# Last stage of a four-stage kernel: the mask written by ScalarE, and four places of its turn reordered

## Chip, cores and metric

One core of a Trainium2 chip runs the whole kernel. The metric is the device time of one execution in microseconds (us); the time before is the median of three runs.

## What is computed

Four stages run one after the other on an activation of 16 sequences x 256 tokens x 128 channels: a recurrent attention, a gated feed-forward net, a full attention, and, as the last stage, six layers of local attention with a feed-forward net. Only the last stage changes. For each layer and each sequence it does:

```python
x = x + local_attention(shift_tokens(x)) @ Wo       # 16 heads of 64, windows of 32
x = x + ffn(layer_norm(x))                          # gelu gate, 341 hidden
# attention: q, k are L2-normalised and turned by rotary tables; a query of a window sees
# its own window and the one before (64 keys):
mask = (it < jb) | (it > jb + w) | (jb == -1)
sim = where(mask, -max, einsum('bhwie,bhwje->bhwij', bq, bk2) * 8)
attn = softmax(sim);  out = einsum('bhwij,bhwje->bhwie', attn, bv2)
# shift_tokens: the upper 64 channels are moved by one token, with a zero at the first
```

## The kernel before

The last stage works through 96 units (six layers x 16 sequences), called n, in a software pipeline of 100 turns, called f. In one turn each engine runs its own list, written out by hand: the first projections of unit f, the last ones and the norms of f-1, the scores and softmax of f-2, the weighted sum and the residual of f-3, the feed-forward net of f-4. Engines meet through semaphores alone, and each engine runs its list in order, so an instruction that waits holds all that stands behind it.

Channels lie on the partitions. Keys and queries are made in eight chunks (`project`, 128 x 512, in banks 0 and 1 in turn). ScalarE squares each chunk (`squares`), GpSimd adds the two halves (`add_halves`), and a product on TensorE with 0/1 weights sums them (`sum_squares`, bank 7). ScalarE turns the sums into reciprocal roots (`norm_rsqrt`: Ln, Exp, Square), VectorE refines them (`norm_weight`, `norm_factor`, `norm_split`, with `norm_high` on ScalarE between), and TensorE spreads them (`spread_norms`). VectorE multiplies each chunk by the rotary tables (`rotary_products`), GpSimd adds the two products (`rotary_sums`, one for each chunk), and SyncE moves queries and keys into their places by 8 DMAs each (`place_queries`, `place_keys`). `rotary_sums` of chunk 0 waits for the key DMAs of the unit before.

The scores of a unit come in two halves h (`scores`, banks 2 and 3): first the mask is put there by eight bf16 products with an identity, then 64 products add the scores. VectorE takes the maximum (`softmax_maximum`) and subtracts it (`softmax_shift`), which frees the banks. GpSimd scales (`scale_shifted`), ScalarE takes the exponential (`softmax_exp`), VectorE sums, GpSimd divides (`softmax_scale`), VectorE transposes. `token_products` makes the values of eight windows (w = 0 to 7, banks 4 and 5), which ScalarE copies out (`read_products`); product 2 goes to the bank of product 0 and waits until ScalarE has read product 0. `attention` is the weighted sum, in two halves. The tokens pass through bank 6: `read_tokens` copies them shifted to SBUF, `split_high_tokens` rounds them, and `split_low_tokens` on VectorE takes the difference.

At the first unit of a layer, ScalarE also writes the rotary tables (`tables`), four of them between `norm_rsqrt` and `softmax_exp`; two turns later TensorE computes `head_matrices` behind the second half of `attention`.

TensorE's list between its tokens and the token products, before:

```python
ffn_up(f - 4, 0); ffn_up(f - 4, 1); scores(f - 2, 0)
project(f - 1, 5); attention(f - 3, 0); project(f - 1, 6); ffn_up(f - 4, 2)
project(f - 1, 7); scores(f - 2, 1); sum_squares(f - 1, 1); attention(f - 3, 1)
token_products(f - 2, 0); project(f, 0, 1); token_products(f - 2, 1); ...
```

## Time and profile before

| | |
|---|---|
| median of 3 runs | 4238.78 us (4233.77 to 4241.29) |
| the profiled execution | 4246.35 us, of it 4244.5 us span |
| TensorE busy over the span | 3910.8 us (92%), VectorE 3529.0 (83%), ScalarE 2638.6 (62%), GpSimd 2381.6 (56%) |
| last stage | from 1325 us (first projection) to the end |
| dearest lines of TensorE | token products 757.9 us, projections 720.7, scores 403.7, weighted sums 373.6, mask 151.7 |

A line of the profile names an engine, the line of the code, the output and the inputs, and how often it ran. "Idle before" is the time in which the engine had nothing to do before these instructions, and what ended it. In the timeline "x8" are eight instructions merged, and the second number runs from the start of the first to the end of the last; matmuls are pipelined, so the distance between starts says what a group costs. "PEld" is TensorE's loading of weights.

### The profile page before, as it was taken

The page shows a single profiled execution, that of the slowest core. Times are in us where ns is not written, and L with a number is a line of the kernel's source. Part 1 is how long each engine was busy: PE and PEld are TensorE (multiplying, and loading weights), DVE is VectorE, ACT ScalarE, POOL GpSimd, SP SyncE. Part 2 cuts the span into 40 slices and gives each one's busy share as a digit, 9 for nine tenths or more (in the row PEclk, how much of TensorE's full clock was granted, in tenths as well). Part 3 has the DMA queues.
Part 4 walks back from the last instruction along what each step waited for, and adds up shares of the span by engine and source line. Part 5 has one row for each costly group of instructions (what it writes and reads, how often), then busy time and mean ns, then how long its engine had stood idle before and what let it go on. Part 6 is the DMA issues. An engine that isn't in the chain of part 4 may idle for free.

```text
span 4244.5 us, 120128 instructions
## 1 busy us (share of the span) xinstructions
PE 3910.8 (92%) x48128; PEld 2747.8 (65%) x48128; DVE 3529.0 (83%) x5537; ACT 2638.6 (62%) x5550; POOL 2381.6 (56%) x2045
## 2 busy tenths in 40 slices
PE   3457999999995999999999999999999999999998
PEld 1225776767764676667766676667766676667666
DVE  6875556777776899989998899989998899989897
ACT  3543336666664666666667666666666666666665
POOL 0111001000003787878888788878888787878785
PEclk7678999999997999999999999999999999999999
DMA  3000000000001333333332333333332333333332
GB/s 104 0 0 1 1 1 1 1 0 0 0 1 40 76 90 82 69 76 88 78 78 65 79 88 81 70 75 94 73 81 62 81 87 81 71 73 72 91 77 65
DMA packets 264482, 238.94 MB, mean 56 GB/s; under 512 B 31524, under 2 KB 260136, under 8 KB 263208
## 3 DMA queue, kind: packets, MB, share of 16 engines
q1 hardware_dynamic: 263976, 231.82, 23.5%
q8 instruction: 363, 5.95, 0.6%
q14 instruction: 143, 1.17, 0.1%
HBM read 26.20 MB, written 4.19 MB: 7 GB/s over the span
## 4 chain that ended last, share of the span: by engine, by line
PE 73%; DVE 12%; ACT 7%; issue 3%; SPq 2%; POOL 1%; DMA 1%; DVEq 0%; ACTq 0%; POOLq 0%
PE bank L1977 14%; PE bank L1910 13%; PE bank L1995 8%; PE bank L1950 7%; PE bank L2037 5%; PE bank L854 5%; ACT arena L1129 3%; PE bank L2050 2%; PE bank L1943 2%; DVE arena L1016 2%; PE bank L1921 2%; DVE arena L1026 2%; PE bank L1254 1%; SPq L2151 1%; PE bank L1245 1%
## 5 line engine op out<-in xcount | busy, mean ns | idle before, releaser
L1448 DVE TENSOR_TENSOR arena<-bank,tab 128x1024 f32<-128x1024 f32 x768 | 935.5, 1219 | 193.0 <-ACT arena L1680 138.8
L1835 POOL TENSOR_TENSOR arena<-arena 128x512 f32<-128x512 f32 x768 | 1010.7, 1332 | 49.6 <-DMA arena<-arena 44.9
L1680 ACT ACTIVATE arena<-bank 128x512 f32<-128x512 f32 x768 | 457.9, 596 | 538.9 <-PE bank L1910 530.1
L1977 PE MATMUL bank<-m_vo,arena 128*32 128x512 f32 x6144 | 757.9, 599 | 17.4 <-DVE arena L1541 11.1
L1910 PE MATMUL bank<-x_split,wqk_split 128*128 128x256 f32 x4608 | 720.7, 299 | 34.9 <-DVE arena L1448 21.0
L1910 PEld LDWEIGHTS bank<-x_split,wqk_split 128*128 128x128 f32 x4608 | 605.6, 192 | 184.3 <-issue 93.9
L1843 POOL TENSOR_TENSOR arena<-arena 128x256 f32<-128x256 f32 x768 | 558.6, 739 | 159.4 <-ACT arena L1680 158.7
L1704 ACT ACTIVATE arena<-bank 128x512 f32<-128x512 f32 x768 | 456.8, 596 | 186.9 <-PE bank L1977 184.2
L1852 POOL TENSOR_TENSOR arena<-arena 128x1024 f32<-128x1024 f32 x192 | 372.4, 1940 | 263.2 <-DVE arena L1496 263.2
L1187 POOL TENSOR_TENSOR x_all<-x_all,arena 128x256 f32<-128x256 f32 x16 | 11.6, 727 | 836.5 <-DVE arena L1008 836.5
L1858 POOL TENSOR_TENSOR arena<-arena 128x1024 f32<-128x1024 f32 x192 | 373.5, 1946 | 127.0 <-DVE arena L1509 126.7
L1950 PE MATMUL bank<-arena 128*32 128x128 f32 x12288 | 403.7, 273 | 0.0
L1995 PE MATMUL bank<-arena 128*32 128x128 f32 x12288 | 373.6, 274 | 0.6 <-issue 0.5
L1950 PEld LDWEIGHTS bank<-arena 128*32 128x32 f32 x12288 | 345.6, 110 | 36.9 <-issue 0.5
L1995 PEld LDWEIGHTS bank<-arena 128*32 128x32 f32 x12288 | 332.7, 110 | 32.5 <-issue 2.0
L1977 PEld LDWEIGHTS bank<-m_vo,arena 128*32 128x32 f32 x6144 | 159.5, 109 | 260.1 <-ACT arena L1704 140.6
L1129 ACT ACTIVATE arena<-bank,arena 128x256 f32<-128x256 f32 x512 | 235.4, 472 | 130.9 <-DVE arena L1016 128.7
L2037 PE MATMUL bank<-arena,w 128*128 128x256 f32 (+1 forms) x1152 | 282.0, 381 | 0.8 <-ACT arena L1735 0.8
L1516 DVE STREAM_TRANSPOSE arena<-arena 128x1024 f32<-128x1024 f32 x192 | 235.1, 1224 | 25.8 <-POOL arena L1858 25.8
L1490 DVE TENSOR_REDUCE arena<-bank 128x16 f32<-128x1024 f32 x192 | 234.1, 1219 | 12.0 <-PE bank L1950 4.1
L1484 DVE TENSOR_TENSOR arena<-arena,bank 128x1024 f32<-128x1024 f32 x192 | 232.1, 1209 | 3.0 <-PE bank L1932 3.0
L1496 DVE TENSOR_TENSOR arena<-bank,arena 128x1024 f32<-128x1024 f32 x192 | 233.0, 1214 | 0.0
(258 smaller groups left out, 7159.4 us busy)
## 6 DMA issues: line engine op xcount, KB each, us to landing
arena<-arena SPq DMA_DIRECT2D x1536, 128.0 KB, 2.5
wqk_stage<-in_wqk SPq DMA_DIRECT2D x6, 1024.0 KB, 8.6
out_x<-x_all SPq DMA_DIRECT2D x7, 512.0 KB, 6.0
wvt<-in_wvt SPq DMA_DIRECT2D x6, 512.0 KB, 4.4
wo<-in_wo SPq DMA_DIRECT2D x6, 512.0 KB, 5.5
arena<-in_wbh SPq DMA_DIRECT2D x1, 2048.0 KB, 9.7
w<-in_w SPq DMA_DIRECT2D x6, 341.0 KB, 5.9
wqk_stage<-out_x SPq DMA_DIRECT2D x2, 512.0 KB, 5.0
```

Source lines behind the costliest of these rows:

```text
L1448: nc.vector.tensor_tensor(d_t[c % KS].rearrange("p k h t -> p k (h t)"), bank[c % 2][:, :].unsqueeze(1).to_broadcast([P, 2, 2 * T]), tab[: ...
L1680: nc.scalar.activation(d_sq[i % 4].rearrange("p h t -> p (h t)"), bank[c % 2][:, :], ACT.Square).then_inc(s_sq, 1)
L1704: nc.scalar.activation(d_u[:, 1 + w, :, :], bank[U_BANK[w]][:, :].rearrange("p (a c) -> p a c", a=QUADS), ACT.Copy).then_inc(s_uev, 1)
L1835: nc.gpsimd.tensor_tensor(d_rot[i // 4][:, i % 4, :, :], t[:, :, 0, :], t[:, :, 1, :], ALU.add).then_inc(s_ad, 1)
L1843: nc.gpsimd.tensor_tensor(sq[:, 0, :], sq[:, 0, :], sq[:, 1, :], ALU.add).then_inc(s_sa, 1)
L1852: nc.gpsimd.tensor_tensor(e, e, factor.to_broadcast([P, WPT, QUADS, 2 * WIN]), ALU.mult).then_inc(s_rm, 1)
L1858: nc.gpsimd.tensor_tensor(d_e[h], d_e[h], d_inv[h].unsqueeze(2).to_broadcast([P, 4 * QUADS, 2 * WIN]), ALU.mult)\
L1910: last = nc.tensor.matmul(bank[c % 2][:, h * T:(h + 1) * T], wqk_split[:, i, wp, h, :], x_split[:, n % 2, xp, :], start=(q == 0), stop=(q ...
L1950: last = nc.tensor.matmul(bank[2 + b][g * WIN:(g + 1) * WIN, (2 * v + a) * P:(2 * v + a + 1) * P], d_q[:, a, g, at:at + WIN], d_k[:, a, g, ...
L1977: last = nc.tensor.matmul(bank[U_BANK[w]][g * WIN:(g + 1) * WIN, :], d_xt[n % 3][:, w * WIN:(w + 1) * WIN], m_vo[:, 4 * g:4 * g + 4, :].re ...
L1995: last = nc.tensor.matmul(bank[6][v * WIN:(v + 1) * WIN, h * C:(h + 1) * C], d_pt[h][:, at, :], d_u[:, WPT * h + v + z, r, :], start=(r == ...
L2037: last = nc.tensor.matmul(bank[UP_BANK[c]][0:m, half * T:(half + 1) * T], w1_of(n)[:, first + c * P:first + c * P + m], d_xn, start=True, ...
```

## The change

ScalarE writes the mask into the two score banks with one copy of 128 x 1024 for each half, instead of TensorE's eight bf16 products; TensorE's eight products stay for the very first half alone. `scores` now waits for this copy. The copy for half 1 stands in ScalarE's list behind `squares` of chunk 6, that for half 0 of the next unit behind the second `softmax_exp`. `split_low_tokens` reads the tokens from bank 6 (two instructions of 64 partitions, the upper one shifted) and stands second in VectorE's list. `softmax_shift` of half 0 stands ahead of the rotary product of chunk 5, and the last two `ffn_gate` and `residual` move up. On TensorE the second half of `attention` stands ahead of `project` of chunk 7. On ScalarE `squares` of chunk 7 stands behind all of `ffn_gelu`. On GpSimd `add_halves` of chunk 7 stands behind `rotary_sums` of chunk 5 and `scale_shifted` of half 0.

```diff
 def split_low_tokens(n):
     dve.wait_ge(s_xh, n + 1)
-    nc.vector.tensor_tensor(x_split[:, n % 2, 1, :], d_xt[n % 3], x_split[:, n % 2, 0, :].bitcast(F32), ALU.subtract)\
-        .then_inc(s_split, 1)
+    at_least(dve, s_proj, CHUNKS * (n - 1))
+    first, second, now = slice(0, C // 2), slice(C // 2, C), n % 2
+    nc.vector.tensor_tensor(x_split[first, now, 1, :], bank[6][first, 0:T],
+                            x_split[first, now, 0, :].bitcast(F32), ALU.subtract)
+    nc.vector.tensor_tensor(x_split[second, now, 1, 1:], bank[6][second, 0:T - 1],
+                            x_split[second, now, 0, 1:].bitcast(F32), ALU.subtract).then_inc(s_split, 1)
...
 for f in range(TURNS_D):            # VectorE
     turn_probabilities(f - 3, 1)
+    split_low_tokens(f)
     rotary_products(f - 1, 3)
     ffn_gate(f - 4, 0)
     rotary_products(f - 1, 4)
     softmax_maximum(f - 2, 0)
-    rotary_products(f - 1, 5)
     softmax_shift(f - 2, 0)
-    rotary_products(f - 1, 6, 7)
+    rotary_products(f - 1, 5, 6)
     ffn_gate(f - 4, 1)
+    ffn_gate(f - 4, 2)
+    rotary_products(f - 1, 7)
+    residual(f - 3)
     softmax_maximum(f - 2, 1)
-    split_low_tokens(f)
-    ffn_gate(f - 4, 2)
     norm_weight(f - 1)
-    residual(f - 3)
     norm_factor(f - 1)
...
+def write_mask(n, h):               # ScalarE
+    if not here(n) or n == 0 and h == 0:
+        return
+    act.wait_ge(s_sub, 2 * n + h)
+    src = mask_bf[:, :, :, :] if h == 0 else mask_bf[:, 1:2, :, :].to_broadcast([P, TPS, 8, 2 * WIN])
+    nc.scalar.activation(psum[:, 2:4, :].rearrange("p b (a k) -> p b a k", k=2 * WIN), src, ACT.Copy).then_inc(s_mask, 1)
...
     squares(f - 1, 5, 6)
+    write_mask(f - 2, 1)
     ffn_gelu(f - 4, 1)
+    ffn_gelu(f - 4, 2)
     squares(f - 1, 7)
-    ffn_gelu(f - 4, 2)
     nc.scalar.preload_act_table_set(EXP_SET)
     norm_rsqrt(f - 1)
...
     softmax_exp(f - 2, 1)
+    write_mask(f - 1, 0)
     read_products(f - 2, 5)
...
     rotary_sums(f - 1, 4)           # GpSimd
-    add_halves(f - 1, 6, 7)
+    add_halves(f - 1, 6)
     rotary_sums(f - 1, 5)
     scale_shifted(f - 2, 0)
+    add_halves(f - 1, 7)
     rotary_sums(f - 1, 6, 7)
...
 def scores(n, h):                   # TensorE
-    at_least(pe, s_sub, 2 * n + h)
+    if n == 0 and h == 0:
+        for b in range(2):
+            for g in range(4):
+                nc.tensor.matmul(bank[2 + b][g * WIN:(g + 1) * WIN, :], ident_bf[:, g * WIN:(g + 1) * WIN],
+                                 mask_bf[:, min(h + b, 1), :, :].rearrange("p a k -> p (a k)"),
+                                 start=True, stop=True, skip_group_check=True, tile_position=(0, g * WIN))
+    else:
+        pe.wait_ge(s_mask, 2 * n + h)
     for b in range(2):
-        for g in range(4):
-            nc.tensor.matmul(bank[2 + b][g * WIN:(g + 1) * WIN, :], ident_bf[:, g * WIN:(g + 1) * WIN],
-                             mask_bf[:, min(h + b, 1), :, :].rearrange("p a k -> p (a k)"),
-                             start=True, stop=True, skip_group_check=True, tile_position=(0, g * WIN))
...
     project(f - 1, 6)
     ffn_up(f - 4, 2)
+    attention(f - 3, 1)
     project(f - 1, 7)
     scores(f - 2, 1)
     sum_squares(f - 1, 1)
-    attention(f - 3, 1)
```

`attention` of half 0 also waits for `s_split`, since it overwrites bank 6; the elements of the low half that no instruction writes now are set to zero once.

## Rows read from the trace of the kernel before

**Rows 1.** The windows view, one stretch: time, then busy time by engine, granted clock.

```profile
3000.00:3300.00 300.00, 294.83 (x4380) 207.07 (x4378) 269.04 (x329) 204.59 (x389) 240.46 (x206) 0.99 0.32 73
```

**Rows 2.** The chain that ended last, in order of time: start, length, what.

```profile
3008.47 0.33 PE bank L1943 x4
3008.80 0.87 PE bank L1950 x32
3009.67 0.21 PE bank L1943 x4
```

**Rows 3.** TensorE in the timeline: start, length, line, operation; one turn and the next.

```profile
3006.30 0.44 PE L1897 MATMUL bank<-ident,x_all 128*128 128x128 f32 x2
...
3018.15 0.61 PE L1921 MATMUL bank<-arena,sel 128*32 128x256 f32 x8
3018.58 1.92 PE L1995 MATMUL bank<-arena 128*32 128x128 f32 x64
3020.33 1.03 PE L1977 MATMUL bank<-m_vo,arena 128*32 128x512 f32 x8
3021.29 1.69 PE L1910 MATMUL bank<-x_split,wqk_split 128*128 128x256 f32 x12
3022.91 1.92 PE L1977 MATMUL bank<-m_vo,arena 128*32 128x512 f32 x16
3024.77 0.44 PE L2006 MATMUL bank<-ident,x_all 128*128 128x128 f32 x2
...
3035.51 0.44 PE L1897 MATMUL bank<-ident,x_all 128*128 128x128 f32 x2
```

**Rows 4.** GpSimd in the timeline, the starts of two turns.

```profile
3007.04 2.52 POOL L1835 TENSOR_TENSOR arena<-arena 128x512 f32<-128x512 f32 x2
...
3037.09 2.51 POOL L1835 TENSOR_TENSOR arena<-arena 128x512 f32<-128x512 f32 x2 [0.86 <-DMA arena<-arena]
...
3044.65 0.74 POOL L1843 TENSOR_TENSOR arena<-arena 128x256 f32<-128x256 f32 x1
...
3046.64 1.29 POOL L1835 TENSOR_TENSOR arena<-arena 128x512 f32<-128x512 f32 x1
3047.89 1.94 POOL L1852 TENSOR_TENSOR arena<-arena 128x1024 f32<-128x1024 f32 x1
3049.78 2.92 POOL L1835 TENSOR_TENSOR arena<-arena 128x512 f32<-128x512 f32 x2
```

**Rows 5.** The waits, whole last stage: total us, times, longest.

```profile
POOL arena L1835 <- DMA arena<-arena: 44.9, 55, 5.1
```

**Rows 6.** ScalarE in the timeline, the same turn.

```profile
3002.10 1.04 ACT L1696 ACTIVATE arena<-arena 128x1024 f32<-128x1024 f32 x1
3004.29 0.60 ACT L1704 ACTIVATE arena<-bank 128x512 f32<-128x512 f32 x1 [1.15 <-PE bank L1977]
...
3008.16 1.28 ACT L1789 ACT_TABLE_LOAD   x1
3009.45 0.47 ACT L1743 ACTIVATE arena<-bank,cols_d 128x256 f32<-128x256 f32 x1
...
3018.83 0.39 ACT L1688 ACTIVATE arena<-bank 128x256 f32<-128x256 f32 x1 [0.51 <-PE bank L1921]
...
3020.65 1.06 ACT L1696 ACTIVATE arena<-arena 128x1024 f32<-128x1024 f32 x1 [0.54 <-POOL arena L1852]
3022.31 0.60 ACT L1680 ACTIVATE arena<-bank 128x512 f32<-128x512 f32 x1 [0.59 <-PE bank L1910]
...
3023.11 0.59 ACT L1704 ACTIVATE arena<-bank 128x512 f32<-128x512 f32 x1
```

**Rows 7.** Groups of instructions, whole last stage: count, busy us, mean ns, idle before.

```profile
L1436 DVE TENSOR_TENSOR x_split<-arena,x_split 128x256 fp32r<-128x256 f32 x96 | 128.5, 1338 | 0.4 <-ACT x_split L1664 0.4
...
L1523 DVE TENSOR_TENSOR x_all<-x_all,bank 128x256 f32<-128x256 f32 x96 | 38.7, 403 | 1.5 <-PE bank L1995 1.5
...
L1764 ACT ACTIVATE tab<-base,qk_cols 128x256 f32<-128x256 f32 x48 | 20.4, 498 | 0.2
```

More of the change, by code:

```diff
@@ L221, in build @@
          a_ge, a_bs_ready, a_bb, a_e_in, a_e, a_er_plus, a_den, a_xr, a_tr2, a_var3, a_y3, a_h2n, a_tr3, a_h2_ready,
-         a_xxx2, a_cr, a_ck, a_relu, a_rk_ready, a_cv, a_er2, a_out, a_tr4, a_x_done) = (sem("a_" + s) for s in (
+         a_xxx2, a_cr, a_ck, a_rk_ready, a_cv, a_er2, a_out, a_tr4, a_x_done) = (sem("a_" + s) for s in (
              "var1 rstd1 var2 rstd2 hn transposed1 h xxx kvr kv ge_in ge cum lncum e_in e er_plus den xr transposed2 var3 rstd3 "
-             "h2n transposed3 h2 xxx2 cr ck relu relu2 cv er2 out transposed4 x_done").split())
+             "h2n transposed3 h2 xxx2 cr ck relu2 cv er2 out transposed4 x_done").split())
         a_fixed = sem("a_fixed")
@@ L1341, in build @@
          s_s, s_sub, s_rm, s_exp, s_inv, s_prob, s_pt, s_u, s_uev, s_at, s_x2, s_x2p, s_xf, s_mean, s_xsq, s_var,
-         d_chain, d_act_chain, s_y2, s_xc, s_xn, s_up, s_gl, s_h, s_ffo, s_x_done, s_m, s_mvo, s_whi, s_wlo, s_tab,
+         d_chain, d_act_chain, s_mask, s_y2, s_xc, s_xn, s_up, s_gl, s_h, s_ffo, s_x_done, s_m, s_mvo, s_whi, s_wlo, s_tab,
          loaded_qk, loaded_sc, loaded_vo, loaded_w1, loaded_w2) = (
@@ L1347, in build @@
                 "s sub rm exp inv prob pt u uev at x2 x2p xf mean xsq var "
-                "chain act_chain y2 xc xn up gl h ffo x_done m mvo whi wlo tab "
+                "chain act_chain mask y2 xc xn up gl h ffo x_done m mvo whi wlo tab "
                 "loaded_qk loaded_sc loaded_vo loaded_w1 loaded_w2").split())
@@ L1354, in build @@
         STORES = ((0, 4), (4, 8), (8, 12), (12, 15), (15, 16))
-        ZEROS = 7
+        ZEROS = 8
         TURNS_D = TOTAL + 4
@@ L1589, in phase_d_vector @@
                 nc.vector.memset(v, 0.0).then_inc(s_zero, 1)
+            nc.vector.memset(x_split[:, :, 1, 0:1].bitcast(F32), 0.0).then_inc(s_zero, 1)
             dve.wait_ge(s_stats, 8)
@@ L1988, in attention @@
                     pe.wait_ge(s_xt, min(n + 4, TOTAL))
+                    pe.wait_ge(s_split, min(n + 4, TOTAL))
                     if n + 3 > LAST:
```

## The prediction

> **What bounds the kernel now.** I first read the windows view of the last stage: in 300 us TensorE is busy for 294.83, VectorE for 269.04, GpSimd for 240.46 and ScalarE for 204.59, at a granted clock of 0.99, which is the upper level of 2.4 GHz [rows 1]. So the reader is to see an engine without gaps, and three others with room of 10, 20 and 32%. The chain that ended last says the same from the other side: nearly every piece of a turn is TensorE's own, with the mask products among them [rows 2]. The timeline of TensorE then gives the turn: from the tokens of one turn to those of the next 3035.51 - 3006.30 = 29.21 us [rows 3]. What is taken from TensorE's list is therefore a gain in full, as long as TensorE doesn't wait for someone in its place. That is the whole question, so I looked for the two hand-overs that the new order tightens: GpSimd's sum of halves ahead of `sum_squares`, and ScalarE's root and exponential behind it. The timelines of GpSimd and ScalarE show how long those chains are [rows 4, 6], and the waits show how often GpSimd itself starts late [rows 5].
>
> I count time in a turn from the tokens (3006.30). `sum_squares` of half 1 starts at 18.15 - 6.30 = 11.85 now [rows 3]; I call its start S.
>
> **Mask off TensorE.** A turn has four groups of four mask products. In the chain a group costs 0.33 or 0.21 us, and the score products behind it 0.87 [rows 2]. The 0.21 is the pure streaming; the 0.12 more of the first group of a half is the change-over from the work ahead, and I expect it to pass on to the score products. The bounds of the gain are 4 x 0.21 = 0.84 and 2 x (0.33 + 0.21) = 1.08 us in a turn; I take 0.87, near the lower, because the change-over is not in the mask. All of it lies on the bounding engine.
>
> **Mask on ScalarE.** No row shows ScalarE writing PSUM. The nearest is its 128 x 1024 exponential, 1.04 us [rows 6]; bounds are 0.6, the 512-wide copy, and 1.2, twice that. I take 1.05, two in a turn, 2.1 us on an engine with 9 us free. Half 0 of the next unit goes behind the second exponential: that ends at 3.14, the copy of value window 5 starts at 4.29 after an idle 1.15 us [rows 6], so the mask just fits in the gap. Cost nothing; the cover is thin, and whatever the copy takes over 1.15 pushes the value copies of windows 5 to 7, for which TensorE waits. Half 1 goes between the square of chunk 6 and the second gelu and waits for `softmax_shift` of half 0. Queued behind it are two gelus, the square of chunk 7, the table load and the roots. The shift has moved ahead of the rotary product of chunk 5, and TensorE has a weighted sum and a projection still to do before it wants the scores, some 2.6 us, so I cost this wait at nothing too (up to 1 us if VectorE were behind).
>
> **Low half from PSUM.** `split_low_tokens` takes 1338 ns for 256 columns, while a VectorE operation of the same width with one input in PSUM takes 403 [rows 7]. The two new instructions should take about 0.4 each: 0.8 in place of 1.34, or at worst 2.7 if they were held up as the old one. They gain VectorE 0.5 us, and TensorE nothing, for it starts `project` of chunk 0 right behind the token product now [rows 3]. The Trainium skill (SBUF — State Buffer, section Who interferes with whom) says that a VectorE instruction with at most one SBUF input doesn't contend with GpSimd, while one with two is held for the whole GpSimd instruction. By it the price is the 0.4, and the old 1338 is explained.
>
> **The weighted sum ahead of the last projection, and GpSimd's order.** The second `attention` costs 20.33 - 18.58 = 1.75 us [rows 3]. It goes from behind S to before it. If TensorE waits for nobody, S moves to 11.85 + 1.75 - 0.87 = 12.73. But `sum_squares` needs all eight half sums, and GpSimd now does chunk 7 only behind one more rotary sum and the scaling of the scores. From its first rotary sum of the turn to the start of the half sum of chunk 6 GpSimd works without a gap: 3044.65 - 3037.09 = 7.56; the half sum takes 0.74, the rotary sum of chunk 5 47.89 - 46.64 = 1.25, the scaling 49.78 - 47.89 = 1.89, the half sum of chunk 7 0.74 [rows 4]. That makes 12.18 us. The first rotary sum starts 7.04 - 6.30 = 0.74 into the turn, or at 37.09 - 35.51 = 1.58 in the next, where the key DMAs were late [rows 3, 4]. Those waits are 44.9 us in 55 of the 96 units [rows 5], 0.47 a turn. So GpSimd starts at 1.21 on average, and S comes at 1.21 + 12.18 = 13.39: TensorE waits 0.66 us, at least 0.19 and in a late turn about 1.0. The bounds are 0.2 (no late DMAs) and 1.1. The DMAs follow `scale_keys`, which follows TensorE's second spread of norms, so I see no reason for them to come sooner.
>
> **What that sum hid.** Between S and token product 2 stood the weighted sum. Without it TensorE wants product 2 at S + 0.43 + 0.96 + 1.62 + 0.93 = S + 3.94 (`sum_squares`, product 0, two projections, product 1) [rows 3]. Product 2 needs the bank of product 0, hence ScalarE's copy of it. In ScalarE's list before that copy stand Ln, Exp and Square, the exponential of half 0, a square and `norm_high`. Ln starts 0.68 behind S (18.83 - 18.15); without its wait of 0.54 for GpSimd the exponential starts 1.28 later (20.65 - 0.54 - 18.83); without the wait of 0.59 the square starts 1.07 behind that; the copy 0.80 later, and takes 0.59 [rows 6]. Together S + 4.42. TensorE waits 0.48. Before there was next to none. Bounds: 0.3, since neighbours on ScalarE overlap by a tenth, and 0.6. I take 0.45.
>
> In the first turn of a layer four table writes of 498 ns [rows 7] stand in that chain. There the wait grows by at most 2 us; some of it was lost before, so I take 1.6, in five turns: 8 us. With the head matrices nothing new is lost in sum: what they lose from the missing cover, product 2 doesn't wait for.
>
> **A rule that speaks against it.** Behind the last square now comes the table load, so it lies between the projection and Ln. The row is 1.28 us, and the gelu behind it starts 0.01 later (3009.45) [rows 6]. At S = 13.39 there are over 2 us for it, and it is hidden. The Trainium skill (ScalarE: Activation LUTs, section What ACT_TABLE_LOAD costs) gives about 2.66 us for a switch, a drain included. By that the load would end at about the time of Ln or 0.5 us past it, and a turn would be up to 0.5 longer; the trace has no such drain, and I leave it to a rival.
>
> **The sum.** A turn: -0.87 + 0.66 + 0.45 = +0.24 us. Late turns of the kernel before lost some 0.05 already, so +0.19; over 92 steady turns +17, with the first turns of layers +8, makes +25. The profiled execution took 4246.35, 1.85 more than its span, and 7.57 more than the median. 4246.35 + 25 = 4271 for a profiled one, and 4238.78 + 25 = 4264 for the median. The mechanism is that the gain of 80 us on the bounding engine comes back as two waits.
>
> **Rivals.** (1) Neither wait takes hold: -0.87 x 95 = -83, 4156. Against it stands GpSimd's gapless chain: it would have to start 0.55 into the turn, and it starts at 0.74 at the earliest. Chance 0.08. (2) One of the two takes hold: only GpSimd's, -0.21 x 92 = -19, 4220; only ScalarE's, -0.42 x 92 = -39, 4200. For it: 0.45 is small against what I add up, and if ScalarE had its copy done by S + 3.94 it would be gone. Chance 0.20. (3) A third wait, at ScalarE: the mask copy longer than its gap of 1.15 us, or Ln held by the load, +0.4 in a turn, +37 more: 4300. It decides from a mask copy of about 1.6 us on, the spare time of value window 5 included, or from a load that ends behind S + 0.68. Chance 0.22. (4) As forecast, 4264; its own range is 4240 to 4290, from the bounds of the two waits. Chance 0.50.
>
> **Numbers.** What a measurement of this kernel can tell from no change is about 0.2%, 8.5 us. Case 4 is slower by more in 0.33, the same in 0.12 and faster in 0.05; cases 1 and 2 are faster, 0.28; case 3 is slower, 0.22. So faster 0.33, same 0.12, slower 0.55. The range goes from 4195, which leaves out case 1 and a part of 2, to 4305.
>
> **What would show it.** In the profile after: score products with no mask products before them, and 0.87 less for them; `sum_squares` starting at 13.4 on average, idle before it put down to GpSimd's L1843 line (its new number), moving with the first rotary sum of the turn; token product 2 waiting 0.4 for ScalarE's copy; mask copies of 1.05; the low half at 0.4 twice; a turn of 29.3 to 29.6. I am wrong if S stands at 12.7 in all turns, if TensorE's gap lies elsewhere, above all at the scores (mask late) or at the value windows 5 to 7, or if the late key DMAs vanish.

## The result, and the profile after

The changed kernel takes 4288.6 us (median of 4 runs, 4281.0 to 4297.5) beside 4240.0 for the kernel before in the same series: ratio 1.0116, 95% interval 1.0104 to 1.0129. The change makes the kernel slower by 1.16%; forecast was 4264, slower by 0.6%. The direction and the range hold; the loss, 48.6 us, is twice the forecast one. The profiled executions took 4297.5 (span 4295.7) and 4246.35 (span 4244.5), so 51.2 us of span have to be found.

The windows view, the same 300 us as in [rows 1]: TensorE is busy for 4.6 us less, VectorE for 4 and GpSimd for 3 less, and ScalarE, which writes the mask now, for 14.5 more. No engine has taken TensorE's place; TensorE has got gaps.

```profile
3000.00:3300.00 300.00, 290.21 (x4195) 197.54 (x4194) 265.05 (x340) 219.05 (x407) 237.25 (x208) 0.99 0.31 71
```

TensorE's timeline, one turn and the start of the `sum_squares` of the next; L1912 are the tokens, L1968 scores, L1936 `sum_squares`, L1995 token products, L2014 weighted sums. The rows answer to [rows 3].

```profile
3007.25 0.44 PE L1912 MATMUL bank<-ident,x_all 128*128 128x128 f32 x2
...
3014.95 1.02 PE L2056 MATMUL bank<-arena,w 128*85 128x256 f32 x4
3015.91 1.95 PE L2014 MATMUL bank<-arena 128*32 128x128 f32 x64
3017.79 0.98 PE L1925 MATMUL bank<-x_split,wqk_split 128*128 128x256 f32 x6
3018.70 1.95 PE L1968 MATMUL bank<-arena 128*32 128x128 f32 x64
3020.47 0.63 PE L1936 MATMUL bank<-arena,sel 128*32 128x256 f32 x8
3020.92 1.04 PE L1995 MATMUL bank<-m_vo,arena 128*32 128x512 f32 x8
3021.89 1.70 PE L1925 MATMUL bank<-x_split,wqk_split 128*128 128x256 f32 x12
3023.51 2.28 PE L1995 MATMUL bank<-m_vo,arena 128*32 128x512 f32 x16
3025.72 0.44 PE L2025 MATMUL bank<-ident,x_all 128*128 128x128 f32 x2
...
3036.48 0.44 PE L1912 MATMUL bank<-ident,x_all 128*128 128x128 f32 x2
...
3050.32 0.64 PE L1936 MATMUL bank<-arena,sel 128*32 128x256 f32 x8 [0.19 <-POOL arena L1857]
```

Three things are to be seen. The score products follow `project` directly, with no mask products. `sum_squares` starts 3020.47 - 3007.25 = 13.22 into the first turn and 3050.32 - 3036.48 = 13.84 into the second, where it waits for GpSimd; before it was 11.85. And token products 1 and 2, merged as x16, need 3025.72 - 3023.51 = 2.21 where they needed 1.86 [rows 3]: product 2 waits 0.35 for ScalarE.

GpSimd in the same two turns (L1849 rotary sums, L1857 half sums), as in [rows 4]:

```profile
3007.99 2.51 POOL L1849 TENSOR_TENSOR arena<-arena 128x512 f32<-128x512 f32 x2
...
3038.10 2.53 POOL L1849 TENSOR_TENSOR arena<-arena 128x512 f32<-128x512 f32 x2 [0.91 <-DMA arena<-arena]
...
3049.52 0.75 POOL L1857 TENSOR_TENSOR arena<-arena 128x256 f32<-128x256 f32 x1
```

The first rotary sum starts 0.74 into the first turn and 1.62 into the second; the last half sum starts at 3049.52, 11.42 behind it, and `sum_squares` follows at 3050.32: 12.22 from the first sum. In this second turn the chain that ended last (start, length, what) runs over this hand-over; the piece of it that [rows 2] show of the kernel before ran on TensorE alone:

```profile
3034.58 3.39 DMA arena<-arena
...
3038.10 2.53 POOL arena L1849 x2
...
3049.57 0.70 POOL arena L1857
...
3050.32 0.68 PE bank L1936 x8
```

ScalarE around the turn's start and behind `sum_squares` (L1702 mask, L1716 copies of values, L1808 table load, L1693 Ln), as in [rows 6]:

```profile
3003.97 1.01 ACT L1702 ACTIVATE bank<-mask_bf 128x1024 f32<-128x1024 bf16 x1
3005.24 0.60 ACT L1716 ACTIVATE arena<-bank 128x512 f32<-128x512 f32 x1 [0.27 <-PE bank L1995]
...
3019.42 1.28 ACT L1808 ACT_TABLE_LOAD   x1
3021.17 0.39 ACT L1693 ACTIVATE arena<-bank 128x256 f32<-128x256 f32 x1 [0.46 <-PE bank L1936]
```

The mask copy for half 0 starts at 3003.97, ends at 3004.98, and the value copy behind it still waits for TensorE (0.27). The table load starts at 3019.42, is done at 3020.70, and Ln still waits 0.46 for `sum_squares`. Neither delays anything here.

The waits of the whole last stage (total us, times, longest), and three groups of instructions (count, busy us, mean ns, idle before):

```profile
POOL arena L1849 <- DMA arena<-arena: 40.8, 45, 5.0
...
PE bank L1995 <- ACT arena L1716: 17.1, 43, 2.0
```

```profile
L1702 ACT ACTIVATE bank<-mask_bf 128x1024 f32<-128x1024 bf16 x191 | 194.0, 1016 | 4.5 <-DVE arena L1500 4.5
...
L1440 DVE TENSOR_TENSOR x_split<-bank,x_split 64x255 fp32r<-64x255 f32 x96 | 40.9, 426 | 1.3
...
L1438 DVE TENSOR_TENSOR x_split<-bank,x_split 64x256 fp32r<-64x256 f32 x96 | 36.8, 384 | 3.8 <-ACT x_split L1669 3.8
```

GpSimd waits for the key DMAs 40.8 us in 45 turns, where it was 44.9 in 55 [rows 5]: they stay late, as forecast.

**Where the 51 us are.** I cut TensorE's timeline of both traces at the tokens of each turn, and took from the same timelines "sum0", the start of GpSimd's first rotary sum, and S, the start of `sum_squares` of half 1, both from the tokens. Turn 16 is the first of the second layer, in which ScalarE writes the tables; turn 18 has the head matrices.

| turns | before, mean us | after, mean us | sum of the differences |
|---|---|---|---|
| steady (70) | 29.26 (S 11.91) | 29.53 (S 13.52) | +18.8 |
| tables (5) | 31.70 (S 11.85) | 34.11 (S 13.92) | +12.1 |
| the turn behind (5) | 29.20 | 29.92 | +3.6 |
| head matrices (5) | 34.53 | 37.04 | +12.5 |
| last turn ahead of a layer | 30.33 | 30.45 | +0.6 |
| the first four turns | | | +7.3 |
| turn 89 | 33.60 | 35.05 | +1.5 |
| start of the stage; the end | 1322.82 | 1318.36 | -4.5; -0.75 |

The sum is 51.2. Over a third is in the steady turns, nearly half (24.6 us) in the ten turns of the tables and the head matrices.

### The profile page after: what moved, and what is told of

It is laid out like the page before. It is cut to its first block, busy times and chain, and to the rows that moved or that the text cites. A ratio compares the mean times of both kernels' runs of the same rounds, so it can differ in the third digit from the quotient of the medians.

```text
span 4295.7 us, 117547 instructions
## 1 busy us (share of the span) xinstructions
PE 3905.7 (91%) x46600; PEld 2690.6 (63%) x46600; DVE 3483.5 (81%) x5634; ACT 2793.1 (65%) x5741; POOL 2342.7 (55%) x2045
## 4 chain that ended last, share of the span: by engine, by line
PE 41%; DVE 21%; ACT 11%; POOL 10%; issue 9%; SPq 4%; DMA 3%; DVEq 0%; ACTq 0%; POOLq 0%
PE bank L1925 6%; POOL arena L1849 6%; PE bank L2014 6%; PE bank L1968 5%; PE bank L1995 5%; PE bank L854 4%; DVE arena L1452 4%; SPq L2170 4%; PE bank L2056 3%; DVE arena L1488 3%; ACT arena L1129 3%; DMA arena<-arena 2%; DVE arena L1016 2%; PE bank L1936 2%; POOL arena L1857 2%
## 5 line engine op out<-in xcount | busy, mean ns | idle before, releaser
L1849 POOL TENSOR_TENSOR arena<-arena 128x512 f32<-128x512 f32 x768 | 977.0, 1289 | 49.2 <-DMA arena<-arena 40.8
L1995 PE MATMUL bank<-m_vo,arena 128*32 128x512 f32 x6144 | 783.9, 606 | 38.2 <-ACT arena L1716 17.1
L1857 POOL TENSOR_TENSOR arena<-arena 128x256 f32<-128x256 f32 x768 | 557.4, 737 | 89.8 <-ACT arena L1685 89.2
L1716 ACT ACTIVATE arena<-bank 128x512 f32<-128x512 f32 x768 | 453.7, 595 | 110.4 <-PE bank L1995 107.5
L2014 PE MATMUL bank<-arena 128*32 128x128 f32 x12288 | 378.3, 275 | 0.9 <-issue 0.9
L1968 PE MATMUL bank<-arena 128*32 128x128 f32 x12288 | 376.1, 274 | 0.3 <-DMA arena<-arena 0.2
L1995 PEld LDWEIGHTS bank<-m_vo,arena 128*32 128x32 f32 x6144 | 160.3, 109 | 319.5 <-ACT arena L1716 170.5
L2014 PEld LDWEIGHTS bank<-arena 128*32 128x32 f32 x12288 | 326.1, 110 | 49.3 <-issue 36.6
L1968 PEld LDWEIGHTS bank<-arena 128*32 128x32 f32 x12288 | 324.7, 110 | 45.2 <-issue 28.2
```

The costliest lines, as they stand in the source:

```text
L1716: nc.scalar.activation(d_u[:, 1 + w, :, :], bank[U_BANK[w]][:, :].rearrange("p (a c) -> p a c", a=QUADS), ACT.Copy).then_inc(s_uev, 1)
L1849: nc.gpsimd.tensor_tensor(d_rot[i // 4][:, i % 4, :, :], t[:, :, 0, :], t[:, :, 1, :], ALU.add).then_inc(s_ad, 1)
L1857: nc.gpsimd.tensor_tensor(sq[:, 0, :], sq[:, 0, :], sq[:, 1, :], ALU.add).then_inc(s_sa, 1)
L1968: last = nc.tensor.matmul(bank[2 + b][g * WIN:(g + 1) * WIN, (2 * v + a) * P:(2 * v + a + 1) * P], d_q[:, a, g, at:at + WIN], d_k[:, a, g, ...
L1995: last = nc.tensor.matmul(bank[U_BANK[w]][g * WIN:(g + 1) * WIN, :], d_xt[n % 3][:, w * WIN:(w + 1) * WIN], m_vo[:, 4 * g:4 * g + 4, :].re ...
L2014: last = nc.tensor.matmul(bank[6][v * WIN:(v + 1) * WIN, h * C:(h + 1) * C], d_pt[h][:, at, :], d_u[:, WPT * h + v + z, r, :], start=(r == ...
```

## The experiments

Times are medians in us; the kernels before that ran beside them had 4240.05, 4241.01 and 4240.61. The turns in this table are worked out in the same way.

| kernel | time | ratio to before, 95% interval | steady turn | S | tables | head matrices |
|---|---|---|---|---|---|---|
| after | 4288.6 | 1.0116 (1.0104 to 1.0129) | 29.53 | 13.52 | 34.11 | 37.04 |
| e1 | 4405.2 | 1.0388 (1.0368 to 1.0408) | 30.92 | 13.48 | 33.74 | 35.29 |
| e2 | 4284.4 | 1.0106 (1.0086 to 1.0126) | 29.38 | 13.38 | 34.20 | 37.04 |
| e3 | 4249.0 | 1.0018 (1.0008 to 1.0027) | 29.34 | 11.88 | 31.65 | 34.54 |
| e4 | 4248.1 | 1.0018 (1.0009 to 1.0028) | 29.29 | 11.83 | 31.76 | 34.56 |
| e5 | 4203.3 | 0.9910 (0.9894 to 0.9927) | 28.77 | 11.25 | 31.46 | 34.08 |
| e6 | 4280.2 | 1.0095 (1.0078 to 1.0112) | 29.42 | 13.41 | 33.75 | 35.97 |
| e7 | 4335.6 | 1.0221 (1.0204 to 1.0238) | 29.97 | 13.97 | 34.35 | 36.65 |
| e8 | 4248.9 | 1.0020 (1.0011 to 1.0030) | 29.26 | 11.90 | 32.10 | 33.64 |
| e9 | 4174.5 | 0.9843 (0.9829 to 0.9856) | 28.47 | 11.09 | 31.47 | 33.51 |
| e10 | 4237.2 | 0.9994 (0.9985 to 1.0003) | 29.22 | 11.85 | 31.68 | 34.25 |
| e11 | 4288.2 | 1.0116 (1.0100 to 1.0131) | 29.46 | 13.45 | 34.07 | 36.02 |

**e1: the weighted sum back behind `sum_squares`,** the rest as after. Is it GpSimd's order that sets S, or TensorE's list?

```diff
-    attention(f - 3, 1)
     project(f - 1, 7)
     scores(f - 2, 1)
     sum_squares(f - 1, 1)
+    attention(f - 3, 1)
```

> The kernel after, with the second weighted sum put back behind the norm sums, as it was; GpSimd's new order stays. My theory says that the norm sums then start where GpSimd lets them, at its first rotary sum + 12.2 us (12.9 into the turn, not the 11.2 that TensorE alone would give), and that the weighted sum, now behind them, hides ScalarE's chain again. So token product 2 waits for nothing, and a turn is 12.9 + 17.4 = 30.3 us, one more than now: about 4370 us. In the head-matrix turns the clock stays at its upper level and they lose nothing beyond that. Rival: GpSimd's order costs nothing and the loss of the change lies in the weighted sum's place. Then this is the kernel before less the masks, 28.5 us a turn and about 4165.

4405, 35 us above what I expected, since S isn't 12.9. It is 13.48, as in after, though TensorE has 1.75 us less to do before it. TensorE's timeline, the tokens and `sum_squares` of one turn:

```profile
3037.71 0.44 PE L1912 MATMUL bank<-ident,x_all 128*128 128x128 f32 x2
...
3050.99 0.64 PE L1936 MATMUL bank<-arena,sel 128*32 128x256 f32 x8 [1.17 <-POOL arena L1857]
```

13.28 into the turn, behind an idle of 1.17 us put down to the half sum. So with the new order on GpSimd its chain alone would hold S at 13.3, whatever TensorE does. That isn't yet the cause of S in the kernel after, where TensorE's own list, with the weighted sum in it, ends at 13.2 too (e2 looks at that side). Given that chain, having the sum ahead of it is right: with GpSimd's new order and the old place of the sum the kernel would lose 1.4 us more in each turn. In the five turns with head matrices the clock stayed at 1.00, as expected.

**e2: the half sum of chunk 7 ahead of the scaling** (the rest as after).

```diff
     rotary_sums(f - 1, 5)
-    scale_shifted(f - 2, 0)
     add_halves(f - 1, 7)
+    scale_shifted(f - 2, 0)
```

> The kernel after, with GpSimd's half sum of chunk 7 ahead of the scaling, behind the rotary sum of chunk 5. My theory: the norm sums start at 13.2 into every turn, whether the key DMAs are late or not; turns of 29.2 us in place of 29.5 on average, 75 of them: 20 us less than the kernel after, about 4267, still slower than before. The scaling ends at 14.9, just ahead of the exponential that needs it. Rival: GpSimd is not what the norm sums wait for in late turns but VectorE's third rotary product; then nothing changes (4288). Second rival: the scaling now comes too late for the exponential, and the wait moves on to token product 2: no gain either.

4284, and the interval overlaps that of after: inconclusive as a gain. S falls from 13.52 to 13.38 only, a steady turn from 29.53 to 29.38. With 1.9 us taken out of GpSimd's chain S stays at 13.2 and above: in the turns that aren't late (first rotary sum at most 1.0 us behind the tokens) it is 13.23, beside 13.25 in after and 13.28 in e1, and TensorE's and VectorE's own work ends there. In the late turns it is 13.48, beside 13.83 in after. So e1 and e2 together show two limits that lie at the same place, and taking away one of them gains little.

**e3: the mask alone,** in the kernel before, with the shift of half 0 ahead of the rotary product of chunk 5 so that the banks are free in time.

```diff
+    write_mask(f - 2, 1)            # ScalarE, behind squares 5, 6
...
+    write_mask(f - 1, 0)            # ScalarE, behind softmax_exp(f - 2, 1)
...
     softmax_maximum(f - 2, 0)       # VectorE
-    rotary_products(f - 1, 5)
     softmax_shift(f - 2, 0)
-    rotary_products(f - 1, 6, 7)
+    rotary_products(f - 1, 5, 6, 7)
```

> The kernel before with the mask on ScalarE alone; of the reordering only the first shift ahead of the rotary product of chunk 5 is taken, since the mask copy needs it. My theory: TensorE saves 0.87, the last projection waits for the rotary product of chunk 5 by 0.4 us, more in turns with late key DMAs; a turn of 28.8 to 29.4, mean 29.05: 4221 us, 0.4% faster than before, with no loss at the layers' first turns (the table writes keep their cover) and none at the norm sums. Rival: ScalarE's mask copies themselves are what costs, through the scores of half 1 or the value windows 5 to 7: then the turn is no shorter than before.

4249, not 4221: 0.87 us a turn are gone from TensorE's list, and the turn is no shorter (29.34, S 11.88). **e4** puts in addition the gate of the feed-forward net behind the rotary product of chunk 4 on VectorE:

```diff
+    rotary_products(f - 1, 4)
     ffn_gate(f - 4, 0)
-    rotary_products(f - 1, 4)
```

> As the run with the mask alone, with the first gate behind the rotary product of chunk 4 on VectorE, so that it no longer waits for the gelu. My theory: the rotary product of chunk 5 ends at 8.2 and not 8.7 into a turn without late DMAs, the last projection waits for nothing there, and the norm sums start at 11.0: a turn of 28.4, in late turns up to 29.2; mean 28.7, about 4195 us, 1.1% faster than before. Rival: the gate wasn't on the path and the same time results as with the mask alone.

4248, far from 4195. In nearly all turns of e4 S is sum0 + 10.55. TensorE's timeline shows what takes the place of the mask: the projection of chunk 7 (L1918) waits for VectorE's rotary product to free its bank.

```profile
3044.16 0.95 PE L1918 MATMUL bank<-x_split,wqk_split 128*128 128x256 f32 x6 [0.55 <-DVE arena L1448]
```

The rotary products in their turn need one of three buffers (`KS = 3`) that GpSimd's sums empty, and product 3 of the same turn, on VectorE, waited for it. The view puts that wait down to GpSimd's rotary sum, L1843:

```profile
3037.64 2.47 DVE L1448 TENSOR_TENSOR arena<-bank,tab 128x1024 f32<-128x1024 f32 x2 [0.77 <-POOL arena L1843]
```

So the late DMAs seem to reach S over GpSimd, the buffers, VectorE and the projections, and the mask products on TensorE had lain in the shadow of that; the next run tries the buffers.

**e5: a fourth buffer** on top of e4.

```diff
-KS = 3
+KS = 4
```

> The mask on ScalarE with the first gate behind the rotary product of chunk 4, and a fourth buffer for rotary products. What the last run showed: the norm sums start at GpSimd's first rotary sum + 10.55 us in nearly every turn, late or not, since rotary product 3 waits for that sum to free one of three buffers. My theory: with four buffers product 3 doesn't wait, the late key DMAs fall off the path, the norm sums start at about 11.1, a turn is 28.5 us where it was 29.3 on average: 0.8 x 85 = 68 us less, about 4180, 1.4% faster than before. Rival: the late DMAs stay on the path, through GpSimd's half sums or the scores themselves, and it stays within 10 us of 4248.

4203, 45 us less than e4, two thirds of the 68 that I expected: the missing buffer was the link. TensorE's timeline, with the wait of the projection gone (sum0 was 1.69 into this turn, a late one):

```profile
2982.17 0.44 PE L1905 MATMUL bank<-ident,x_all 128*128 128x128 f32 x2
...
2990.53 0.97 PE L1918 MATMUL bank<-x_split,wqk_split 128*128 128x256 f32 x6
...
2993.37 0.64 PE L1929 MATMUL bank<-arena,sel 128*32 128x256 f32 x8
...
3010.88 0.44 PE L1905 MATMUL bank<-ident,x_all 128*128 128x128 f32 x2
```

S is 11.20, and the turn 28.71 us.

**e6: the old place of the sum in layer turns alone,** the rest as after: do the layer turns lose because the weighted sum no longer fills (covers) the time in which ScalarE works behind `sum_squares`?

```diff
-    attention(f - 3, 1)
+    layer_turn = here(f) and f % SEQS == 0 or here(f - 2) and (f - 2) % SEQS == 0
+    if not layer_turn:
+        attention(f - 3, 1)
     project(f - 1, 7)
     scores(f - 2, 1)
     sum_squares(f - 1, 1)
+    if layer_turn:
+        attention(f - 3, 1)
```

> The kernel after, with the second weighted sum put back behind the norm sums in eleven turns only: those with the table writes and those with the head matrices. My theory: it covers ScalarE's chain there, TensorE doesn't stand idle, and its granted clock doesn't fall from 1.0 to 0.5; by the run with the sum put back everywhere these turns then take 33.7 in place of 34.1 (five) and 35.3 in place of 37.0 (six): 12 us less than the kernel after, about 4276. Rival: the loss in those turns is ScalarE's copies of the head matrices themselves, which come no sooner: no change, 4288.

4280, 8 us less than after by the medians; the two intervals overlap a little, so the gain rests on the turns. The head turns fall from 37.04 to 35.97, the table turns from 34.11 to 33.75. What is behind it shows in turn 50, which has the head matrices (L2083). First in after, TensorE's timeline and then the windows, whose last three columns are the granted clock, the DMA share and GB/s:

```profile
2836.22 0.64 PE L1936 MATMUL bank<-arena,sel 128*32 128x256 f32 x8 [0.17 <-POOL arena L1857]
...
2839.69 1.94 PE L2083 MATMUL bank<-wo,wvt 64*128 64x128 f32 x16 [1.19 <-ACT m_vo L1785]
2842.31 1.94 PE L1995 MATMUL bank<-m_vo,arena 128*32 128x512 f32 x8 [0.69 <-ACT m_vo L1785]
2844.18 2.93 PE L1925 MATMUL bank<-x_split,wqk_split 128*128 128x256 f32 x12
2847.04 2.30 PE L1995 MATMUL bank<-m_vo,arena 128*32 128x512 f32 x16
```

```profile
2836.00:2840.00 4.00, 2.64 (x30) 1.99 (x27) 2.37 (x5) 3.11 (x7) 2.62 (x3) 1.00 0.03 8
2840.00:2842.00 2.00, 1.63 (x16) 1.33 (x14) 0.00 (x0) 1.06 (x3) 0.00 (x0) 0.76 0.87 192
2842.00:2844.00 2.00, 1.69 (x8) 0.20 (x8) 0.00 (x0) 0.26 (x1) 0.00 (x0) 0.50 0.90 210
...
2846.00:2848.00 2.00, 2.00 (x14) 1.13 (x16) 1.50 (x2) 1.26 (x3) 0.00 (x0) 0.53 0.00 0
2848.00:2850.00 2.00, 2.00 (x24) 0.72 (x17) 1.26 (x3) 1.18 (x3) 0.68 (x1) 1.00 0.00 0
```

TensorE waits 1.19 and 0.69 us for ScalarE's copies of the head matrices (L1785), and the granted clock goes from 1.00 to 0.50, the lower level of 1.2 GHz. By the shares of the windows it falls at about 2841.0, behind the first of the two waits and before the second, and is back at 1.00 at about 2847.9, some 7 us later. In between twelve projection products take 2.86 us instead of 1.62, and a group of eight token products 1.87 instead of 0.97. The same turn of e6, with the weighted sum (L2014) between `sum_squares` and the head matrices, and one of its windows:

```profile
2827.73 0.64 PE L1936 MATMUL bank<-arena,sel 128*32 128x256 f32 x8 [1.56 <-POOL arena L1857]
2828.18 1.93 PE L2014 MATMUL bank<-arena 128*32 128x128 f32 x64
...
2831.95 1.71 PE L2083 MATMUL bank<-wo,wvt 64*128 64x128 f32 x16 [0.19 <-ACT m_vo L1785]
2834.34 1.06 PE L1995 MATMUL bank<-m_vo,arena 128*32 128x512 f32 x8 [0.69 <-ACT m_vo L1785]
2835.34 1.69 PE L1925 MATMUL bank<-x_split,wqk_split 128*128 128x256 f32 x12
```

```profile
2834.00:2836.00 2.00, 1.66 (x13) 0.82 (x14) 0.00 (x0) 0.29 (x1) 0.00 (x0) 1.00 0.89 204
```

Here TensorE waits 1.56 us ahead of `sum_squares`, and 0.19 and 0.69 for the copies; the clock stays at 1.00, and the twelve projection products last 1.69 us, where they last 2.93 in after. From S to the end of the turn it is 21.83 us in turns 34, 50 and 82 of e6, and 23.7 in turns 18, 50, 66 and 82 of after (mean clock 0.86).

The difference of 1.9 us isn't the price of the clock, since e6 has the weighted sum in that stretch and after hasn't. Like with like are two turns of other runs whose TensorE list behind `sum_squares` is that of after: turn 18 of e11 and turn 66 of e7. Both have the same two waits, and their clock stayed at 1.00. Turn 18 of e11, one window from S to its end, and its timeline:

```profile
1863.40:1884.45 21.05, 19.04 (x173) 11.57 (x165) 14.92 (x22) 15.72 (x31) 10.30 (x9) 1.00 0.44 99
```

```profile
1866.84 1.71 PE L2083 MATMUL bank<-wo,wvt 64*128 64x128 f32 x16 [1.19 <-ACT m_vo L1785]
```

So at the upper level the stretch is 21.05 us with the sum gone from it, 0.8 less than in e6, and the fallen clock costs 2.7 us in each of those four turns of after. So without the fall the turns would be shorter with the sum ahead; what the sum does behind `sum_squares` is to keep the clock up more often. Over the traces of all runs, in the five turns with head matrices the clock fell in 18 of 20 turns where the sum stands ahead (after, e2, e7, e11) and in 7 of 45 where it stands behind `sum_squares` (before and the other runs); in the turns with tables in 10 of 20 and in 0 of 45. The waits within the turn don't decide it alone, as e11's turn 18 shows.

In the table turns, too, the cover is worth nothing at the upper level: the turn takes 33.77 in after and 33.75 in e6, for token product 2 waits for ScalarE's tables either way. There the loss is mainly S, 13.92 in place of 11.85; in three of the five turns of after the clock fell as well, for 0.5 to 0.7 us each.

**e7: the mask back on TensorE** in after; nothing else undone.

```diff
-    write_mask(f - 2, 1)            # ScalarE
-    write_mask(f - 1, 0)
...
-    pe.wait_ge(s_mask, 2 * n + h)
+    at_least(pe, s_sub, 2 * n + h)
     for b in range(2):
+        for g in range(4):
+            nc.tensor.matmul(bank[2 + b][g * WIN:(g + 1) * WIN, :], ident_bf[:, g * WIN:(g + 1) * WIN],
+                             mask_bf[:, min(h + b, 1), :, :].rearrange("p a k -> p (a k)"),
+                             start=True, stop=True, skip_group_check=True, tile_position=(0, g * WIN))
```

> The kernel after with the mask back on TensorE (and no mask copies on ScalarE); all reordering stays. My theory: the norm sums move from 13.2 to 13.9 in turns without late DMAs (0.44 for the second half's masks, 0.26 for the first's, whose rest goes into the wait for rotary product 3), and late DMAs up to 0.9 us then cost nothing: a turn of 29.9 where the mean is 29.5, +0.4 x 90 = 36 us, about 4325. Rival: the mask copies are what costs, on ScalarE; then it is faster than the kernel after.

4336, where 4325 was expected. TensorE's timeline, the two tokens and `sum_squares`:

```profile
3000.88 0.44 PE L1910 MATMUL bank<-ident,x_all 128*128 128x128 f32 x2
...
3014.82 0.60 PE L1934 MATMUL bank<-arena,sel 128*32 128x256 f32 x8
...
3030.82 0.44 PE L1910 MATMUL bank<-ident,x_all 128*128 128x128 f32 x2
```

S is 13.94 and the turn 29.94, 0.44 us longer than in after on average (29.97 and 29.53). So the reordering alone costs 95 us, and taking the mask off TensorE gives back 47 of them, a good half of the 0.87 x 95 = 83 that its products take.

**e8: the low half alone** from PSUM, second in VectorE's list, in the kernel before (`attention` of half 0 waits for it, as in after).

```diff
     turn_probabilities(f - 3, 1)
+    split_low_tokens(f)             # two instructions of 64 partitions from bank 6
...
     softmax_maximum(f - 2, 1)
-    split_low_tokens(f)
```

> The kernel before with the low half read from PSUM, second in VectorE's list, and nothing else. My theory: VectorE gains 0.5 us a turn, TensorE has the masks still and doesn't wait for rotary product 3 (it ends at 3.9, projection 5 starts at 4.4): no change, 4240 within 5. Rival: the early place delays the rotary products enough that TensorE waits, 0.2 to 0.4 us a turn, 4260 to 4280.

4249, 8 us slower and not the same: a small miss. The steady turn is unchanged (29.26). The table turns and the ones behind lose 0.4 each, the first four turns about 1.1 each, the head turns gain 0.9. Second in its list, the split stands ahead of the rotary product of chunk 3, for which TensorE waits 0.36 us in the table turns and in those behind them. Of the 0.9 in the head turns 0.6 is the clock, which fell in two of the five head turns of the kernel before and in none of e8.

**e9: all that the runs pointed to,** on top of e5: the mask of half 1 between the squares of chunks 5 and 6, the low half ahead of the second maximum, the scaling ahead of the rotary sum of chunk 5.

```diff
-    squares(f - 1, 5, 6)            # ScalarE
+    squares(f - 1, 5)
     write_mask(f - 2, 1)
+    squares(f - 1, 6)
...
+    split_low_tokens(f)             # VectorE
     softmax_maximum(f - 2, 1)
-    split_low_tokens(f)
...
-    rotary_sums(f - 1, 5)           # GpSimd
     scale_shifted(f - 2, 0)
+    rotary_sums(f - 1, 5)
```

> The kernel with the fourth buffer, and three moves: the mask of half 1 between the squares of chunks 5 and 6, the low half ahead of the second maximum, the scaling ahead of the rotary sum of chunk 5. In the run before the scores of half 1 waited some 0.2 us for the mask copy and projection 0 some 0.24 for the low half. My theory: both waits go, a turn is 28.3 in place of 28.7: about 4165, 1.7% faster than before. Rival: the square of chunk 6 comes later and GpSimd's half sums with it, or the second maximum; then it stays at 4200.

4174.5 (5 runs, 4171.3 to 4177.1), 1.6% faster than before and 2.7% faster than after, 10 us short of the 4165 expected. The windows view of the same 300 us:

```profile
3000.00:3300.00 300.00, 294.26 (x4380) 207.91 (x4370) 277.47 (x338) 227.36 (x418) 247.90 (x213) 1.00 0.32 73
```

Its busy share of TensorE is as in [rows 1], with the mask products gone: the time they took is now turned into shorter turns (28.47).

**e10: the fourth buffer in the kernel before,** and **e11: in after.** In both `KS = 4` is the only edit.

> The kernel before with a fourth buffer for rotary products and nothing else. My theory: TensorE is the bound there and waits for the late DMAs only in a few turns (0.05 us a turn): 0 to 5 us less, 4236, no change that can be measured. Rival: the gain of the run with the fourth buffer (46 us) has nothing to do with the mask, and it comes here too: 4195.

> The kernel after with a fourth buffer for rotary products. My theory: the norm sums in it wait for GpSimd's chain, which starts at the late rotary sum whatever VectorE does: they stay at that sum + 12.2 us, and only turns without late DMAs gain up to 0.2 us: 4280 to 4288. Rival: in late turns it is VectorE's product 3 that holds the norm sums: then all turns are 29.1 and it comes to about 4245.

4237 and 4288: nothing in either. Of the three kernels that got the fourth buffer it pays in one alone, e5, where the mask is gone from TensorE, the sum stands behind `sum_squares` and the gate is later.

## Why the prediction was right, and where it missed

**S and GpSimd's wait.** The chain was right and S nearly so: 12.22 from the first rotary sum to `sum_squares` (12.18 forecast), sum0 1.17 on average (1.21), S 13.52 (13.39). But the value is right in part by luck: GpSimd's chain ends last in the late turns alone, 33 of the 70, and e1 and e2 show a second limit at the same place. Without the wait S is 13.22, not 12.73. Of that 0.49 some 0.34 are change-overs between groups that were not neighbours before (from start to start the third `ffn_up` and `project` of chunk 7 take 0.96 and 0.91, where they took 0.67 and 0.99 as neighbours, and the weighted sum 1.88 instead of 1.75), the rest waits for rotary product 3 (in the first turn shown it ended at 3011.24 on VectorE, and `project` of chunk 5, which needs its bank, started at 3011.38). So GpSimd's wait costs 0.30 over a turn that has already lost 0.49 in its place; together 0.79, forecast 0.66.

**What the sum hid.** Right: 0.35 measured, 0.45 taken, bounds 0.3 and 0.6. Behind S a turn takes 29.53 - 13.52 = 16.01; the forecast was 29.21 - 11.85 - 1.75 + 0.45 = 16.06.

**The late key DMAs** stay, as argued. Where the first rotary sum is late (over 1.0 us into its turn), it follows the S of the turn before by 18.86 us before and by 17.59 after, and the next S follows it by 10.42 and by 12.21. The change shortened the one stretch by 1.27 us, since no weighted sum stands in it any more, and lengthened the other by 1.79. Together they are the distance from one S to the next, 29.28 before and 29.80 after; that this comes near the length of a turn follows from its definition, and doesn't show that the loop over GpSimd and the DMAs sets the turn. In the kernel before it doesn't: 56 of its 70 steady turns have S at 11.85, wherever sum0 lies between 0.7 and 1.6. In after 35 of 70 have it at 13.22 to 13.26, and in the late ones it follows sum0 by 12.2. In e4 it follows sum0 by 10.55 in 87 of 91 turns, and there the loop holds S nearly everywhere.

**Mask off TensorE, -0.87.** The products are gone as forecast, and the steady turn came out at +0.27 where +0.19 was forecast. e3 and e7 limit the term: alone in the kernel before it gains nothing, and in the new order 0.44 of 0.87. "What is taken from TensorE's list is therefore a gain in full, as long as TensorE doesn't wait for someone in its place" stands with its condition, but the hand-over that counts in e3 isn't one of the two that I looked at: it is the projections' wait for a bank, behind VectorE, the buffers, GpSimd and the late DMAs. e4 and e5 show that link, 45 us with one more buffer.

**Mask on ScalarE, no cost.** Right: 1016 ns (1.05 taken), and the value copy behind it still waits for TensorE. **Low half.** 384 and 426 ns in place of 1338, as taken; that its new place costs something (e8, 0.4 us in each table turn and the one behind) was not seen. **The table load.** Right, and rival 3 is out: 1283 ns, and Ln waits 0.46 for TensorE behind it.

**The step that failed** is the price of the layer turns: "In the first turn of a layer ... I take 1.6, in five turns: 8 us. With the head matrices nothing new is lost in sum". Measured are 12.1 and 12.5 us, 24.6 in place of 8 and some 1.9 of the steady term, so 15 of the 26 us missing. What the runs show in its place:

- *Table turns, 12.1.* S is 2.07 later, 10.4 us in five turns. At the upper clock ScalarE's tables set the time from S to token product 2, and it is 19.86 us from S to the turn's end after and 19.85 before, so whatever is put ahead of S is lost in full there. I had priced only what the sum had hidden, and let the mask's gain stand beside it. The other 1.7 us are the clock, which fell in three of the five.
- *Head turns, 12.5.* S is 1.69 later on average, 8.4 us in five turns. From S to the end it is 21.05 us at the upper clock (e11, e7) and 22.09 before, so 5.2 us come back, and 3.2 us of loss would be left at that clock. The other 9.3 us are the clock, 12.3 in after less 3.0 in the kernel before, where it fell in two of the turns.

So the clock, which was in no term of mine, makes 11 of these 24.6 us. The spread of the runs goes with it, too: the fastest execution of after, 4281.0, had a mean granted clock of 0.964, the profiled and slowest one, 4297.5, had 0.960. The rest of what is missing: 5.5 us in the steady turns, 2.3 in the turns ahead of a layer and behind the tables, 7.3 in the first four, 1.3 in turn 89, less 5.3 at the two ends.

**Open:** the split of the 7.3 us at the stage's start, where the stage itself starts 4.5 us sooner; a part may be the clock, which is granted at 0.50, 0.50, 0.76 and 0.95 in the first four turns after and at 0.62, 0.62, 0.83 and 1.00 before. Of the 0.72 in each turn behind the tables e8 shows 0.4 for the low half's place; the rest has no run of its own. Why the clock falls in some turns and not in others with the same waits isn't shown: in e6 it fell in head turns 18 and 66 (mean 0.93 from S on), as in the kernel before, and not in the other three.

## What to carry to other kernels

An engine that is busy for 98% isn't proof that work taken off it is gained: first follow each of its list's waits one link further (here a bank, a ring of three buffers, a late DMA), since removed work may have lain in the shadow of such a chain; the mask off TensorE gained nothing by itself (e3, e4), and with one more buffer, which alone gained nothing either (e10), 38 us on the kernel before (e5). A group that covers another engine's chain is priced in every kind of turn, the rare ones with longer chains above all: ten turns of 100 held nearly half of the loss here. And an idle bounding engine can cost more than its idle time: where the clock fell behind it, a turn here lost 2.7 us more. When two engines' chains end at the same place, one experiment that shortens one of them doesn't name the cause; it takes both.

## What the runs showed of the hardware

- **The granted clock of TensorE fell within a turn.** Behind an idle time of 1.19 us it went from 1.00 to 0.50, and back some 7 us later (after, turn 50); products took 1.8 to 1.9 times as long, and such turns 2.7 us longer than the ones with the same waits in which it stayed at 1.00 (e11 turn 18, e7 turn 66). In e6 idle times of 1.56, 0.19 and 0.69 us with products between them left it at 1.00 in turn 50.
- **ScalarE writes 128 x 1024 fp32 to PSUM from bf16 in 1016 ns** (191 times), no dearer than its exponential of that size in SBUF, 1.04 us.
- **VectorE's difference with one input in PSUM:** 384 and 426 ns for 64 partitions of 256. With both inputs in SBUF the same 256 columns took 1338 ns before [rows 7], and 1518 where ScalarE wrote the mask and nothing of it was changed (the group in e3):

```profile
L1436 DVE TENSOR_TENSOR x_split<-arena,x_split 128x256 fp32r<-128x256 f32 x96 | 145.8, 1518 | 0.4 <-ACT x_split L1663 0.4
```

  Its 96 instructions show what it waits for: in both traces the first, beside which GpSimd ran nothing, took 424 and 426 ns, and the other 95 ended some 0.28 us behind the end of the GpSimd instruction that ran when they started. By the Trainium skill (SBUF — State Buffer, section Who interferes with whom) a VectorE instruction with at most one SBUF input doesn't contend with GpSimd, and one with two contends with a GpSimd instruction that reads SBUF; the runs agree.
- **What a group on TensorE costs depends on its neighbours:** the third `ffn_up` took 0.67 us ahead of a projection and 0.96 ahead of the weighted sum, the weighted sum 1.75 and 1.88 in its two places.
